# Graph attention front: source halves first, softmax in pieces, gathers before scatters, first rows normalised in the aggregation

## The reference

```python
x_norm = layernorm(x, ln_g, ln_b)                      # x has been layernormed once already
q = (x_norm @ Wq + bq); k = (x_norm @ Wk + bk); v = (x_norm @ Wv + bv)   # 8 heads of 64
ws = einsum('ehd,ehd->eh', q[origin], k[destination]) * SCALE * edge_weights
e = exp(ws - segment_max(ws, origin)[origin])
att = e / (segment_sum(e, origin)[origin] + 1e-16)
values = segment_sum(att[:, :, None] * v[destination], origin)
x = x + x_norm0 + (values @ W1 + b1) @ W2 + b2         # then the first feed-forward layer
```

## Time and profile before

| | us |
|---|---|
| median of 3 runs (2661.26 to 2667.1) | 2661.51 |
| the profiled execution | 2660.17 |
| its span in the profile | 2658.3 |
| TensorE busy in it (89%) | 2376.4 |
| VectorE busy in it (66%) | 1767.0 |

### The profile page before, as it was taken

How to read it: one execution, slowest core, us unless ns; L and a number is a source line. 1 busy time by engine, 2 the same in 40 slices (tenths; PEclk the granted TensorE clock), 3 DMA queues, 4 the chain that set the end, 5 groups by cost and what they waited for, 6 DMA issues and landing times. The chain is left out here.

```text
span 2658.3 us, 33629 instructions
## 1 busy us (share of the span) xinstructions
PE 2376.4 (89%) x10818; PEld 1868.2 (70%) x10818; DVE 1767.0 (66%) x4156; ACT 1131.6 (43%) x2077; POOL 684.6 (26%) x644
## 2 busy tenths in 40 slices
PE   6588868599999999999958999999978599999998
PEld 4466646377777777777746888888866477777776
DVE  7357667677777777777545675555555377777775
ACT  6354312335444454544433222222223666665651
POOL 5433231311121112211022212122222433333320
PEclk9699979799999999999979999999989699999999
DMA  4111221311221212211063343433436566666631
GB/s 153 46 39 33 49 73 68 103 64 60 84 93 51 95 52 92 81 62 60 32 191 113 127 146 125 136 127 131 135 121 195 107 139 146 162 140 167 147 98 48
DMA packets 156034, 271.90 MB, mean 102 GB/s; under 512 B 35442, under 2 KB 36082, under 8 KB 155638
## 3 DMA queue, kind: packets, MB, share of 16 engines
q1 hardware_dynamic: 122918, 203.00, 23.2%
q0 software_dynamic: 32976, 67.19, 11.2%
HBM read 185.82 MB, written 100.41 MB: 108 GB/s over the span
## 5 line engine op out<-in xcount | busy, mean ns | idle before, releaser
L1192 POOL TENSOR_TENSOR d_rs<-d_ve,net_half_neg 128x4 f32<-128x4 f32 x60 | 70.4, 1173 | 508.9 <-DVE d_ve L1239 422.3
L2135 ACT ACTIVATE conv_h<-conv_h 128x512 f32<-128x512 f32 x79 | 50.0, 632 | 309.6 <-DVE conv_h L2087 296.8
L2582 POOL DMA_INDIRECT next_own<-message,d_at x79 | 128.2, 1623 | 163.1 <-DMA next_own<-own 141.2
L2057 DVE TENSOR_TENSOR conv_yl<-conv_pty,conv_yh 128x512 fp32r<-128x512 f32 x79 | 54.6, 692 | 150.3 <-ACT conv_yh L2131 140.0
L1198 POOL DMA_INDIRECT d_val<-values,net_slot_s x79 | 85.8, 1086 | 217.3 <-DVE d_x L1316 88.3
L68 PE MATMUL conv_p<-conv_w_hi,conv_yh 128*128 128x512 f32 x316 | 132.9, 421 | 0.6 <-DVE conv_yl L2057 0.6
L1512 ACT ACTIVATE d_act_out<-d_pa 128x512 f32<-128x512 f32 (+1 forms) x80 | 45.9, 574 | 198.7 <-PE d_pa L70 198.7
L68 PE MATMUL d_po<-shared_wq_hi,d_hh 128*128 128x512 f32 x316 | 129.0, 408 | 1.5
L68 PE MATMUL d_pc<-d_xh,shared_wv_hi 128*128 128x512 f32 (+1 forms) x320 | 129.6, 405 | 0.0
L68 PE MATMUL d_pa<-d_xh,shared_wk_hi 128*128 128x512 f32 (+1 forms) x320 | 128.4, 401 | 0.0
L68 PE MATMUL conv_p<-conv_w_hi,conv_hh 128*128 128x512 f32 x316 | 124.8, 395 | 2.3 <-DVE conv_hl L2057 1.9
(11 more groups left out here) (553 smaller groups left out, 7196.6 us busy)
## 6 DMA issues: line engine op xcount, KB each, us to landing
y<-d_y SPq DMA_DIRECT2D x79, 256.0 KB
conv_yin<-y SPq DMA_DIRECT2D x79, 256.0 KB, 2.8
h<-conv_h SPq DMA_DIRECT2D x79, 256.0 KB, 2.0
own<-conv_own SPq DMA_DIRECT2D x79, 256.0 KB
next_own<-own SPq DMA_DIRECT2D x79, 256.0 KB, 4.3
next_x<-y SPq DMA_DIRECT2D x79, 256.0 KB, 3.2
out<-d_res SPq DMA_DIRECT2D x79, 256.0 KB, 2.3
early_x<-in_x SPq DMA_DIRECT2D x10, 1024.0 KB
```

Source lines behind the costliest of these rows:

```text
L1192: pool.tensor_tensor(rs[n][:], ve[n][:], k.half_neg[:, 0:T], ALU.pow).then_inc(pow_done[n], 1)
L2057: v.tensor_tensor(lo[:, t % 2, :], bank[t % 2][:], hi[:, t % 2, :].bitcast(F32), ALU.subtract)\
L2135: act_.activation(h[:, t, :], h[:, t, :], ACT.Relu).then_inc(h_made, 1)
L2582: pool.indirect_dma_start(own[n][:, t, :], None, k.message2[:, :], bass.IndirectOffsetOnAxis(ap=at[:, t:t + 1], axis=0), bounds_check=EP + ...
```

## The change

`Softmax.parts` becomes `part(v, g, n)` in four pieces: 0 is the scan and the addition, 1 and 2 are the reciprocal of 256 columns each, 3 the three multiplications. `low` counts on a semaphore of its own, and `levels` part 2 waits for it. DVE puts pieces 0 to 2 into the k loop of the next group and piece 3 behind it; `compare` moves up into the k loop, ahead of the scores; the statistics of the next source rows move from before the k loop to after its first chunk; the low parts of the next source rows are interleaved with the statistics of the next destination rows. ACT's `high` moves from ahead of the q evictions to the q loop one group later. In the first group the source tiles are split before the destination rows are normalised, and two more PSUM banks take their turns. POOL issues the next gathers ahead of the scatters, which come in blocks of five. In the last group, `parts` no longer stands ahead of the flags. In the aggregation `ah` and `al` have two buffers, the low parts come one per tile, and the last group makes the statistics and the layernorm of the first 1,024 rows of the next phase.

```diff
 class Softmax:
-    STEPS, LEVELS, PARTS = 15, 7, 13
+    STEPS, LEVELS = 14, 7
...
+            if g:
+                v.wait_ge(self.low_made, 2 * g)
             s(v.tensor_tensor(self.expo[:, 1, :], self.score[:], m[:, 1:GR + 1], ALU.subtract))
...
+    def part(self, v, g, n):
+        if n == 0:
+            v.wait_ge(self.exp_done, g + 1)
+            s.link(v.tensor_tensor_scan(self.total[:, 1:GR + 1], old, new, self.total[:, 0:1], ALU.mult, ALU.add))
+            s.link(v.tensor_scalar(scale, self.total[:, 1:GR + 1], 1e-16, None, ALU.add))
+        elif n < 3:
+            half = slice((n - 1) * GR // 2, n * GR // 2)
+            s.link(v.reciprocal(scale[:, half], scale[:, half]))
+        else:
+            s(v.tensor_tensor(new[low], new[low], scale[low], ALU.mult))
+            s.link(v.tensor_tensor(new[up], old[up], self.total[up, 0:GR], ALU.mult))
+            s(v.tensor_tensor(new[up], new[up], scale[up], ALU.mult))
...
 project_edges, gpsimd:
-        for g in range(EG):
-            gather(g, "s")
-            powers(g, "s")
-            gather(g, "d")
-            powers(g, "d")
...
+        for x in "sd":
+            gather(0, x)
+        for x in "sd":
+            powers(0, x)
+        for g in range(EG - 1):
+            gather(g + 1, "s")
+            scatter(g, 0)
+            gather(g + 1, "d")
+            powers(g + 1, "s")
+            scatter(g, 1)
+            powers(g + 1, "d")
         scatter_slots("d", range(ET))
...
+    def bank(g, x, t):
+        return (tr + pp)[t] if g == 0 and x == "s" else tr[t % 2]
...
 project_edges, vector:
+        s = statistics(v, 0, "d")
+        split_lo(v, 0, "s", 0)
+        split_lo(v, 0, "s", 1)
+        statistics2(v, 0, "d", s)
+        split_lo(v, 0, "s", 2)
+        statistics3(v, 0, "d", s)
+        split_lo(v, 0, "s", 3)
...
             for t in range(T):
-                split_lo(v, g, "d", t, t % 2)
-                if g >= 2 and t == 0:
+                split_lo(v, g, "d", t)
+                if g >= 2 and t == 2:
                     soft.low(v, g - 2)
-                if g and t:
-                    soft.levels(v, g - 1, same["s"], t - 1)
-            if not last:
-                s = statistics(v, g + 1, "s")
-            else:
+                if g and t != 2:
+                    soft.levels(v, g - 1, same["s"], min(t, 2))
+            if last:
                 place("d")
-                soft.parts(v, g - 1)
...
+                if not last and cc == 0:
+                    s = statistics(v, g + 1, "s")
...
+                if g and cc:
+                    soft.part(v, g - 1, cc - 1)
+                if cc >= 2:
+                    compare(g, cc - 2)
+            if last:
+                soft.part(v, g - 1, 3)
+            else:
+                compare(g, 2)
+                split_lo(v, g + 1, "s", 0)
             v.wait_ge(attr_out, g + 1)
             v.wait_ge(score_done, 4 * g + 4 + 2)
...
                 widen(g + 1)
-                s = statistics(v, g + 1, "d")
...
+                statistics0(v, g + 1, "d", range(2))
+                split_lo(v, g + 1, "s", 1)
+                s = statistics(v, g + 1, "d", 2)
+                split_lo(v, g + 1, "s", 2)
+                statistics2(v, g + 1, "d", s)
+                if g:
+                    soft.part(v, g - 1, 3)
+                statistics3(v, g + 1, "d", s)
+                split_lo(v, g + 1, "s", 3)
...
-                if g:
-                    soft.parts(v, g - 1)
...
 project_edges, scalar:
+                if g >= 2 and cc == 1:
+                    soft.high(act_, g - 2)
...
+                if not last and cc == KC - 1:
+                    for t in range(T):
+                        norm(act_, g + 1, "d", t)
+                if last and cc == 0:
+                    soft.high(act_, g - 1)
...
-            if g and not last:
-                soft.high(act_, g - 1)
...
 aggregate_values:
-    ah, al = c.sb("ah", [P, KC, GR], F32R), c.sb("al", [P, KC, GR], F32R)
+    ah, al = ([c.sb(f"{n}{i}", [P, KC, GR], F32R) for i in range(2)] for n in ("ah", "al"))
...
                     scan(g + 1, t)
+                    if t:
+                        low(g + 1, t - 1)
...
+                if g == EG - 1:
+                    if t < 2:
+                        statistics(0, t)
+                    if t == 1:
+                        statistics(0, 2)
+                    if t >= 2:
+                        statistics(1, t - 2)
+                    if t == 2:
+                        scales(0)
             if g < EG - 1:
-                for cc in range(KC):
-                    low(g + 1, cc)
+                low(g + 1, KC - 1)
+        statistics(1, 2)
+        scales(1)
...
-                if cc == 0:
-                    act_.wait_ge(row_out, 4 * g + 2)
+                if cc == 0 and g >= 2:
+                    act_.wait_ge(row_done, 4 * g - 4)
...
+        early.norm(act_, 0)
...
 dense0_phase, vector:
-            front0(0, 0)
+            v.sem_inc(stats[0], 2 * NSTAT)
+            v.sem_inc(shift_made[0], 4)
             constants()
...
+            add(1, 1, 0)
+            add(1, 1, 1)
             for t in range(T):
-                add(1, 1, t)
+                low(0, 0, t)
+            add(1, 1, 2)
+            add(1, 1, 3)
             front1_begin(0, 1)
+            front1(0, 1)
             v.wait_ge(consts, 8)
-            routing(0, {})
+            routing(0, {4: lambda: front1_end(1)})
...
```

More of the change, by code:

```diff
@@ L746, in _ @@
                     diagonal(flagged[g], cc + 2)
-                if last and cc == 3:
-                    soft.low(v, g - 1)
+                if not last and cc == 0:
+                    s = statistics(v, g + 1, "s")
                 if not last and cc == 1:
@@ L771, in _, with w12_split @@
                     number_ranks(range(10, ET))
-                if g:
-                    soft.parts(v, g - 1)
         v.wait_ge(score_out, EG + 1)
-        for part in range(3):
+        for part in range(2):
             soft.levels(v, EG - 1, same["s"], part)
-        for cc in range(KC):
+        soft.low(v, EG - 2)
+        soft.levels(v, EG - 1, same["s"], 2)
+        def w12_split(cc):
             v.wait_ge(w12_high, cc + 1)
@@ L780, in _ @@
              .then_inc(w12_low, 1)
-        soft.parts(v, EG - 1)
+        w12_split(0)
+        w12_split(1)
+        for part in range(4):
+            soft.part(v, EG - 1, part)
+        w12_split(2)
+        w12_split(3)
         soft.low(v, EG - 1)
         v.wait_ge(w12_low, KC)
+        v.wait_ge(soft.low_made, 2 * EG)
     def norm(act_, g, x, t):
@@ L801, in copy_flags, with w12_split @@
             act_.activation(same[x][:, i * GR + 1:(i + 1) * GR + 1], pk[n % 2][:], ACT.Copy).then_inc(flags_ready, 1)
+        def w12_split(cc):
+            act_.wait_ge(w12_in, 16)
+            act_.activation(hi["wq"][:, cc, :], w12[:, cc, :], ACT.Copy).then_inc(w12_high, 1)
         act_.sem_inc(v_out, 4)
-        for x in "sd":
-            for t in range(T):
-                norm(act_, 0, x, t)
         for t in range(T):
-            split_hi(act_, 0, "s", t, t % 2)
+            norm(act_, 0, "s", t)
+        for t in range(T):
+            split_hi(act_, 0, "s", t)
+        for t in range(T):
+            norm(act_, 0, "d", t)
         for g in range(EG):
@@ L843, in _ @@
                                 bias=bias[:, 2, cc:cc + 1]).then_inc(v_out, 1)
-                if not last and cc >= 2:
-                    norm(act_, g + 1, "d", 2 * cc - 4)
-                    norm(act_, g + 1, "d", 2 * cc - 3)
-                if last:
-                    act_.wait_ge(w12_in, 16)
-                    act_.activation(hi["wq"][:, cc, :], w12[:, cc, :], ACT.Copy).then_inc(w12_high, 1)
-            if g and not last:
-                soft.high(act_, g - 1)
-        soft.exponents(act_, EG - 1)
+                if not last and cc == KC - 1:
+                    for t in range(T):
+                        norm(act_, g + 1, "d", t)
+                if last and cc == 0:
+                    soft.high(act_, g - 1)
+                if last and cc < 2:
+                    w12_split(2 * cc)
+                    w12_split(2 * cc + 1)
+                if last and cc == 2:
+                    soft.exponents(act_, EG - 1)
         soft.high(act_, EG - 1)
@@ L1009, in _ @@
                     .then_inc(early.weight_low[n], 1)
+        for n in range(2):
+            pool.wait_ge(early.stats, early.STATS * (n + 1))
+            pool.tensor_tensor(early.rs[n][:], early.ve[n][:], k.half_neg[:, 0:T], ALU.pow).then_inc(early.pow_done, 1)
         for n, _, _, _, _ in coming:
@@ L1214, in _ @@
             pool.sem_inc(x1_made, 4)
-            for t in range(T):
-                gather(0, t)
-            power(0, 0)
+            pool.sem_inc(pow_done[0], 2)
+            for g in range(2):
+                for t in range(T):
+                    gather(g, t)
             power(0, 1)
-            power(1, 0)
-            for t in range(T):
```

(2 more changed lines are left out.)

131 lines of the change are left out of this document (63 added, 68 removed).

## The result

The changed kernel takes 2598.53 us (median of 4, 2596.0 to 2599.98) beside 2661.58 us for the kernel before (4 runs, 2661.26 to 2667.1). The ratio is 0.9756, 95% interval 0.9744 to 0.9768. The profiled execution took 2598.54 us with a span of 2596.4 us. 2600 was forecast.

A forecast was written before the change was run, and what follows sets the result against it. The projection was taken as bound by engines waiting for each other, not by one engine or memory. Projection -52.1, stalls +6, aggregation -12.5, tail +0.7, next phase -2.6 give -60.5 from 2660.17: 2599.7, predicted 2600, range 2586 to 2624.

The forecast's parts named there:

- the last group: Projection's end, last k start to aggregation: flags no longer behind `parts`, 37.5 us instead of 51.1, -13.6.
- the allowance: Projection: +6 us charged for remote waits of ScalarE that may come back, taken between none and as before.
- First gathers, first q loop: Projection start: first q matmul at 82.2 us instead of 92.90, -10.7; first q loop 17.1 us without its stall, -6.1.
- k to q: Projection, k loop start to next q loop start: -4.3 us in group 0, +3.9 and +5.7 in 1 and 2, -1.4 in 3.
- (b): VectorE's list becomes the bound: source low parts 4 to 5 us later per group, aggregation gains half; 2624 us, chance 0.15.
- q loops: Projection, groups 1 to 4: ScalarE meets no softmax block ahead of its q evictions; gains 4.4, 8.6, 10.9 and 1.7, -25.6 us.
- Rival (d): Projection: the softmax only moves its wait from q evictions to k loops, one to one; 2622 us, chance 0.03.
- Stalls of ACT: Projection: ScalarE's remote waits, 18.6 us in four before, up to 14 reaching TensorE; bounds none or as before, +6 taken.
- the load of slots 3: done at 31, hidden, with 5 us to spare: Last projection group: twenty slot scatters start at about 2 us, take 26, then the load ends at 31, costing nothing.
- Aggregation and tail: Aggregation: two buffers take the low-part waits off five boundaries, -12.5 us; its tail ends later by statistics and power, +0.7.
- Next phase: Phase after the aggregation: group 1 gets statistics before the routing, so a turn that waited 2.87 us is on time, -2.6.

## Why the prediction was right

*Range and sign.* 2600 was forecast and 2598.53 measured. Six of the terms of the sum lie within 1 us of the table. That the total is off by no more than 1.5 us is in part luck: the last group came 3.5 us worse than its term with the allowance, and the other terms 4.8 us better together. On the second chip the same change brings 57.9 us, and not 63.

*First gathers, first q loop.* -17.3 us in place of -16.8. The first loop took its expected 17.1 us, with no remote wait in it (16.0 to 17.5 us in the variants). Of the change here nothing was undone by itself.

*k to q.* 34.7 us where 35.3 was worked out, with the waits at the third turn, 3.3 and 4.2 us, where they were said to be. The two undoings of source halves and softmax pieces change exactly these numbers, to 37.4 and 38.6 and to 29.4. Group 0 kept 33.9 us where 32.6 was worked out, 1.3 us too little charged. The rival of a new bound on VectorE (b) had a true core, a list that is too long in two groups; its price was in the sum already.

*q loops.* -27.0 for -25.6. With the block back (21.6 us in groups 2 and 3) 15.5 of it go, so that much comes from the softmax in pieces. The other 11.5 us are not shown by an undoing. In sum, though not group by group, they are as long as the three remote waits of ScalarE at the q evictions of these groups in the kernel before (4.1, 3.7 and 3.7 us), which the changed kernel doesn't have. GpSimd's order may be what took them away, but it was undone only on the chip whose traces have no such wait. Rival (d), that the softmax only moves its wait, is two thirds true in groups 1 to 4: 15.5 us saved, 10.6 paid. It is false for the last group, where the block had stood ahead of the diagonals and its 7.3 us go for good.

*Stalls of ACT.* The allowance of +6 came out as some +9 in one place, the last group, where 38.1 us without scatters is close to the 37.5 of the sum. On a second chip it was none, and another 2.4 us stood there instead: the step "the load of slots 3: done at 31, hidden, with 5 us to spare" is wrong in its end. The load was done at 32.2 us behind the k start, but the phase also waits for GpSimd's DRAIN, which ends 9.2 us behind the start of the last scatter and which the sum had at nothing; with the barrier that makes 10.7 us in six runs on that chip. The +6 itself was a choice between two bounds, and that it fits is luck: it lies between two things, a stand of 9 us and an end of 2.4 us, that it did not know apart. The prediction had held the 7.1 us of the earlier trace rows against a rule of the Trainium skill (Runtime: NRT & Kernel Launch, Instruction fetch mechanics), by which such a fetch is mostly hidden. The traces show nothing that disagrees with that rule: the 7.1 us, too, end with a late rise of TensorE's counter, and in the stand of 10.1 us no block of instructions starts on its way.

*Aggregation and tail.* -12.8 for -11.8, and shown by its undoing, 12.3 us. TensorE is the bound there with 13.04 us per group, as worked out (13.1).

*Next phase.* -4.0 for -2.6, but not by the step that was named. The turn that waited 2.87 us waits 0.19 (timeline of TensorE in the changed kernel):

```profile
460.22 0.66 PE L1710 MATMUL d_ptr<-net_ident,d_xf 128*128 128x128 f32 x4 [0.19 <-ACT d_xf L1587]
```

Counted from the first turn of the phase it comes at 27.2 us where it came at 27.6, so the wait that went was paid ahead of it, and 0.4 us are won there. At the last of the 20 groups 0.9 us are won (812.2 us behind the first turn, where it was 813.1). The other 3.1 us lie in phases that the change doesn't touch, within the 7.3 us by which the variants differ over the whole stretch.

*What stays open.* Why the counter rises late in ScalarE's stand. The stand was not there without the scatters, ends 2.4 and 3.5 us behind the start of the last of them in two kernels, and does not occur on the other chip. The records of the semaphore put it at the rise of the counter and not at a fetch of instructions. What holds the rise up, the indirect transfers by themselves or together with the recording of the trace, no row tells.

## What to carry to other kernels

When work is moved off one wait, sum the list of its engine over the whole period and find the next thing due in it: here the q loops won 27.0 us and the k loops of groups 1 and 2 paid 8.3, and both could be worked out from the durations before. Indirect transfers that nothing needs soon still have an end that a barrier waits for; look for the instruction with which the issuing engine ends its part, here GpSimd's DRAIN, and don't take only the landing of the load behind them. And run the reference kernel on the chip of the variant before a few microseconds are put down to an edit.

## What the hardware showed that was not expected

- One program, two chips: the kernel before took 2661.11 us on one and 2651.15 us on the other, the changed one 2598.53 us in the first comparison and 2593.28 us on the second chip. In the profiles of the changed kernel all but the last group agrees to 0.3 us up to there; the 6.5 us of difference in it is the stand of ScalarE beside the row of indirect transfers, present in one and absent in the other.
- On the first chip ScalarE, which takes no part in a row of 20 indirect scatters (1.34 us from one to the next in the mean), stood 10.1 us beside it for a counter of TensorE that rose 10.1 us behind its matmul; without the row it waits 0.92 us at the same place. No trace of the second chip has such a wait.
- From the issue of the last scatter to the first matmul of the next phase it is 10.7 us on the second chip, in the six runs in which nothing else is later: 9.2 us until GpSimd's DRAIN ends and 1.5 for the barrier. The load of 40 KB behind the scatters is long done by then.
- The aggregation gives an earlier start back in part: 99.7 us with the scatters moved into it (start 325.66), 97.2 in the changed kernel (start 328.62). The windows of the two, 95 us from 2.62 us behind the start, first the changed kernel's on the second chip, then the other's, have 2.6 us more of TensorE's busy time at a lower mean clock:

```profile
331.24:426.24 95.00, 67.21 (x277) 52.65 (x277) 76.66 (x123) 24.49 (x42) 25.25 (x28) 0.88 0.40 144
```

```profile
328.28:423.28 95.00, 69.84 (x275) 54.14 (x274) 75.90 (x120) 23.10 (x40) 40.96 (x42) 0.82 0.41 142
```
